# A split-precision expert loop whose h tile is written in place into a PSUM bank

## What is computed

```python
def expert_step(acc, w):
    wg, wu, wd = w                       # 128x512, 128x512, 512x128
    h = jax.nn.silu(x @ wg) * (x @ wu)
    return (acc + h @ wd, None)
acc, _ = jax.lax.scan(expert_step, jnp.zeros_like(x), (Wg, Wu, Wd))
```

## Time and profile before

| | |
|---|---|
| time, median of 3 runs | 551.64 us (551.34 to 551.76) |
| time of the profiled execution | 551.68 us |
| its span | 549.9 us, 8707 instructions |
| TensorE matmuls busy | 541.6 us (98%), 2643 instructions |
| VectorE busy | 442.1 us (80%), 978 |
| ScalarE busy | 347.7 us (63%), 626 |
| GpSimd busy | 164.3 us (30%), 205 |
| granted TensorE clock | 0.999 of full |

### The profile page before, as it was taken

How to read it: one execution, slowest core, us unless ns; L and a number is a source line. 1 busy time by engine, 2 the same in 40 slices (tenths; PEclk the granted TensorE clock), 3 DMA queues, 4 the chain that set the end, 5 groups by cost and what they waited for, 6 DMA issues and landing times.

```text
span 549.9 us, 8707 instructions
## 1 busy us (share of the span) xinstructions
PE 541.6 (98%) x2643; PEld 467.0 (85%) x2643; DVE 442.1 (80%) x978; ACT 347.7 (63%) x626; POOL 164.3 (30%) x205
## 2 busy tenths in 40 slices
PE   9999999999999999999999999999999999999996
PEld 5788888888888888888888888888888888888885
DVE  5689887898768997789877988779976888778666
ACT  6797676756675566755658466675667555655554
POOL 6567784216203360034501335022520033001001
PEclk9999999999999999999999999999999999999999
DMA  6233320210102101111101111021010200010000
GB/s 191 78 121 111 107 65 3 77 45 13 60 0 78 58 20 39 42 35 59 49 10 63 35 41 57 1 76 40 20 40 0 78 20 21 19 40 0 21 0 21
DMA packets 29329, 25.47 MB, mean 46 GB/s; under 512 B 3169, under 2 KB 21986, under 8 KB 29282
## 3 DMA queue, kind: packets, MB, share of 16 engines
q1 hardware_dynamic: 27984, 24.19, 13.8%
q10 hardware_dynamic: 1298, 0.72, 0.5%
HBM read 15.73 MB, written 9.18 MB: 45 GB/s over the span
## 4 chain that ended last, share of the span: by engine, by line
PE 95%; ACT 2%; DVE 1%; issue 1%; POOLq 0%; POOL 0%; DVEq 0%; ACTq 0%
PE gate_ps L1064 10%; PE acc_ps L1067 10%; PE acc_ps L1064 10%; PE gate_ps L1065 10%; PE gate_ps L1067 10%; PE acc_ps L1065 10%; PE up_ps L1064 10%; PE up_ps L1065 10%; PE up_ps L1067 10%; PE att_ps L1121 1%; PE att_ps L1109 1%; PE up_ps L1167 1%; ACT h_hi L627 1%; PE att_ps L1097 1%; PE gate_ps L1167 0%
## 5 line engine op out<-in xcount | busy, mean ns | idle before, releaser
L650 ACT ACTIVATE gs<-gate_ps 128x512 f32<-128x512 f32 x255 | 152.0, 596 | 175.4 <-PE gate_ps L1067 172.3
L874 DVE TENSOR_TENSOR h<-gs,up_ps 128x512 f32<-128x512 f32 x255 | 174.1, 683 | 92.9 <-PE up_ps L1067 90.0
L861 DVE TENSOR_TENSOR h_lo<-h,h_hi 128x512 fp32r<-128x512 f32 x255 | 193.8, 760 | 0.1
L627 ACT ACTIVATE h_hi<-h 128x512 fp32r<-128x512 f32 x255 | 158.9, 623 | 9.4 <-DVE h L874 8.9
L1064 PE MATMUL gate_ps<-x1nT_hi,wg_hi 128*128 128x512 f32 (+1 forms) x254 | 98.7, 388 | 1.7 <-ACT wg_hi L580 0.9
L1067 PE MATMUL acc_ps<-h_lo,wd_hi 128*128 128x512 f32 x254 | 96.4, 379 | 0.2 <-DVE h_lo L861 0.2
L1064 PE MATMUL acc_ps<-h_hi,wd_hi 128*128 128x512 f32 x254 | 96.3, 379 | 0.0
L1065 PE MATMUL acc_ps<-h_hi,wd_lo 128*128 128x512 f32 x254 | 96.3, 379 | 0.0
L1065 PE MATMUL up_ps<-x1nT_hi,wu_lo 128*128 128x512 f32 (+1 forms) x254 | 96.1, 378 | 0.0
L1067 PE MATMUL gate_ps<-x1nT_lo,wg_hi 128*128 128x512 f32 (+1 forms) x254 | 96.1, 378 | 0.0
L1064 PE MATMUL up_ps<-x1nT_hi,wu_hi 128*128 128x512 f32 (+1 forms) x254 | 96.1, 378 | 0.0
(11 more groups left out here) (233 smaller groups left out, 492.8 us busy)
## 6 DMA issues: line engine op xcount, KB each, us to landing
w_raw<-in_L_ffn_Wg_dram SPq DMA_DIRECT2D x8, 256.0 KB, 2.8
w_raw<-in_L_ffn_Wu_dram SPq DMA_DIRECT2D x8, 256.0 KB, 2.6
w_raw<-in_L_ffn_Wd_dram SPq DMA_DIRECT2D x8, 256.0 KB, 3.5
x_in<-in_L_attn_x_dram SPq DMA_DIRECT2D x7, 256.0 KB, 2.9
t_dram_x1n<-t_blk_x1n SPq DMA_DIRECT2D x7, 256.0 KB, 2.0
t_out_x1n<-t_dram_x1n SPq DMA_DIRECT2D x28, 64.0 KB, 1.9
t_dram_acc<-t_blk_acc SPq DMA_DIRECT2D x7, 256.0 KB, 2.3
t_out_acc<-t_dram_acc SPq DMA_DIRECT2D x28, 64.0 KB, 2.0
```

The source lines that it names most:

```text
L627: act.activation(h_hi[s % NH][:, :], h[s % NGU][:, :], ACT.Copy).then_inc(s_hhi, 1)
L650: act.activation(gs[q][:, :], gate_ps[q][:, :], ACT.Silu).then_inc(s_silu, 1)
L861: dve.tensor_tensor(h_lo[s % NH][:, :], h[s % NGU][:, :], h_hi[s % NH][:, :].bitcast(F32), ALU.subtract).then_inc(s_hlo, 1)
L874: dve.tensor_tensor(h[q][:, :], gs[q][:, :], up_ps[q][:, :], ALU.mult).then_inc(s_h, 1)
```

## The change

h loses its tiles in SBUF. VectorE writes gs * up back into the PSUM bank from which it read up. ScalarE makes h_hi and VectorE makes h_lo from that bank. The bank is then free for the next up when h_lo is made, so TensorE's wait before up is on s_hlo instead of s_h; VectorE's waits before h (until h_hi and h_lo of the tile's last user are made) go away.

In the last step the second half of up goes to the attention's bank att_ps, for which TensorE doesn't wait, and the first half of the last sum to up_ps[(STEPS - 3) % NGU].

The splits of the weights are moved: expert e's three tiles are copied at steps 4 (e - 2), + 1 and + 2, and their low parts made one step later. Those of experts 0 and 1 (m up to 5) are made before the first step. GpSimd no longer waits for s_hlo. TensorE waits for the low parts of Wg and of Wu separately, each before its first product.

```diff
-LO_AT = {4: 1, 5: 2, 6: 3, 7: 4, 8: 6, 9: 7, 10: 8, 11: 10, 12: 11, 13: 12, 14: 14, 15: 15, 16: 16, 17: 17, 18: 20,
-         19: 21, 20: 24, 21: 25, 22: 26, 23: 27}
-HI_AT = {m: when - 1 for m, when in LO_AT.items() if m > 5}
+FIRST = 2
...
+        HI_AT = {m: FT * (m // 3 - FIRST) + m % 3 for m in range(3 * FIRST, NW)}
+        LO_AT = {m: when + 1 for m, when in HI_AT.items()}
...
-        h = [sb(f"h{i}", [P, N]) for i in range(NGU)]
...
-        last_up_ps = [up_ps[(STEPS - 1) % NGU], up_ps[(STEPS - 3) % NGU]]
-        last_acc_ps = [att_ps, gate_ps[(STEPS - 2) % NGU]]
+        last_up_ps = [up_ps[(STEPS - 1) % NGU], att_ps]
+        last_acc_ps = [up_ps[(STEPS - 3) % NGU], gate_ps[(STEPS - 2) % NGU]]
...
                     for m, when in LO_AT.items():
                         if first and when == s:
-
-                            pool.wait_ge(s_hlo, s)
                             split_lo(pool, m)
...
             pool.wait_ge(s_f_x1n, J)
-            split_lo(pool, 2)
-            split_lo(pool, 3)
+            for m in range(2, 3 * FIRST):
+                split_lo(pool, m)
...
-                act.activation(h_hi[s % NH][:, :], h[s % NGU][:, :], ACT.Copy).then_inc(s_hhi, 1)
+                act.activation(h_hi[s % NH][:, :], up_ps[s % NGU][:, :], ACT.Copy).then_inc(s_hhi, 1)
...
-                dve.tensor_tensor(h_lo[s % NH][:, :], h[s % NGU][:, :], h_hi[s % NH][:, :].bitcast(F32),
+                dve.tensor_tensor(h_lo[s % NH][:, :], up_ps[s % NGU][:, :], h_hi[s % NH][:, :].bitcast(F32),
                                   ALU.subtract).then_inc(s_hlo, 1)
...
-                    if not (first and s < NGU):
-                        dve.wait_ge(s_hhi, t - since(s, NGU) + 1)
-                        dve.wait_ge(s_hlo, t - since(s, NGU) + 1)
                     q = s % NGU
-                    dve.tensor_tensor(h[q][:, :], gs[q][:, :], up_ps[q][:, :], ALU.mult).then_inc(s_h, 1)
+
+                    dve.tensor_tensor(up_ps[q][:, :], gs[q][:, :], up_ps[q][:, :], ALU.mult).then_inc(s_h, 1)
...
-                if first and f == 0:
-                    pe.wait_ge(s_whi, 3 * e + 2)
-                    pe.wait_ge(s_wlo, 3 * e + 2)
-                for k, ps, s_done, s_free in ((0, gate_ps[q], s_gate, s_silu), (1, up_ps[q], s_up, s_h)):
+                for k, ps, s_done, s_free in ((0, gate_ps[q], s_gate, s_silu), (1, up_ps[q], s_up, s_hlo)):
+                    if first and f == 0:
+                        pe.wait_ge(s_wlo, 3 * e + k + 1)
                     if not (first and s < NGU):
                         pe.wait_ge(s_free, t - since(s, NGU) + 1)
...
-                                                  (1, last_up_ps[i], s_up, s_h)):
-                        pe.wait_ge(s_free, t - 3 + 1 + i)
+                                                  (1, last_up_ps[i], s_up, s_hlo)):
+                        if ps is not att_ps:
+                            pe.wait_ge(s_free, t - 3 + 1 + i)
```

More of the change, by code:

```diff
@@ L639, in last_step @@
                     act.wait_ge(s_h, t + 1 + i)
-                    act.activation(h_hi[r][:, half], h[q][:, half], ACT.Copy).then_inc(s_hhi, 1)
+                    act.activation(h_hi[r][:, half], last_up_ps[i][:, half], ACT.Copy).then_inc(s_hhi, 1)
             def body(b, par, first, nxt, last):
@@ L889, in last_step @@
                     dve.wait_ge(s_silu, t + 1 + i)
-                    dve.tensor_tensor(h[q][:, half], gs[q][:, half], last_up_ps[i][:, half],
+                    dve.tensor_tensor(last_up_ps[i][:, half], gs[q][:, half], last_up_ps[i][:, half],
                                       ALU.mult).then_inc(s_h, 1)
@@ L894, in last_step @@
                     dve.wait_ge(s_hhi, t + 1 + i)
-                    dve.tensor_tensor(h_lo[r][:, half], h[q][:, half], h_hi[r][:, half].bitcast(F32),
+                    dve.tensor_tensor(h_lo[r][:, half], last_up_ps[i][:, half], h_hi[r][:, half].bitcast(F32),
                                       ALU.subtract).then_inc(s_hlo, 1)
```

## The result

The changed kernel takes 563.02 us (median of four runs, 562.79 to 563.20) against 551.63 us; the ratio is 1.0207, with a 95% interval of 1.0189 to 1.0225. The forecast was 563.3 us, with a range of 559.2 to 566.5.

The account below looks back on a forecast made before the run. TensorE was taken as the bound, busy 541.6 of 549.9 us. Image-start stalls 5.4, step-5 stalls 6.1 and first image 0.1 summed to +11.6 us on 551.7, giving 563.3 us, range 559.2 to 566.5.

Parts of the forecast that it names:

- The stalls at s=0 and s=1: First two steps of images 1 to 7: up waits for h_lo of two steps earlier, 14 times, 5.4 us in all.
- The stalls at s=5: Step 5 of images 1 to 6: up waits for h_lo made late by ScalarE's table loads, six times, 6.1 us.
- What a stall costs beyond its lateness: At each TensorE wait: 0.08 us from release to start, plus 0.07 us before the next matmul.
- The price of PSUM: h written to and read from PSUM: taken as no cost; upper bound 0.08 us per stall, 1.6 us for 20.
- the page's rule: Trainium skill's VectorE access overhead, about 125 ns on PSUM against 60 on SBUF: 2.6 us over 20 stalls, time 566.0.
- h_lo without collisions: With one SBUF operand h_lo no longer waits for GpSimd splits: mean from 760 to about 685 ns, none near 1.39 us.
- The first image: Waits that go against new waits of up there: sum +0.1 us, bounds -1.0 to +1.
- up(3) and up(7): First image, up at steps 3 and 7 waits for h_lo: starts 27.25, 1.17 us late, and 36.54, 1.45 us late.
- A dear write: Rival, chance 0.04: writing into the PSUM bank being read doubles h to 1.2 us; about 595 us.
- only one kind of stall: Rival, chance 0.07: only the image-start waits or only the step-5 waits of up appear, 5.4 or 6.1 us; 557.4 us.
- Faster: Rival, chance 0.04: up's wait for h_lo never binds, three first-image waits are gain, 2.65 us; 549.0 us.
- unchanged: Rival, chance 0.02: gains and stalls cancel within 0.2%, 1.1 us, needing stalls of 2.7 us in all.

Follow-up runs that it names:

- the wait alone: Kernel before with one word changed: TensorE's up waits for s_hlo instead of s_h, h stays in SBUF, splits as before; 564.31 us, ratio 1.0230.
- the run with the splits alone: Kernel before with only the new weight-split times, no s_hlo wait on GpSimd, separate TensorE waits; h stays in SBUF; 551.83 us, ratio 1.0003.

## Why the prediction was right, point by point

- *The stalls at s=0 and s=1.* Forecast 14 x 0.385 = 5.4 us; the trace has 7 x (0.40 + 0.35) = 5.3 us, and choosing banks by t took away 5.24. Right, in mechanism and size.
- *The stalls at s=5.* Forecast 6 x 1.02 = 6.1 us; the trace has 6 x 1.00. Identity for Exp took away 7.66, of which 6.0 are these and 1.5 is up(7)'s stall of the first image. Right, and the table loads are the cause.
- *What a stall costs beyond its lateness.* Forecast 0.08 for the release and 0.07 behind it; measured 0.05 and 0.10. The two errors cancel, which is luck: I took the 0.07 from a matmul released by a split, while the one released by h_lo in the same rows, 0.48 us long instead of 0.38, already showed the 0.10.
- *The price of PSUM.* Taken as 0, at most 0.08 per stall. h went from 683 to 693 ns and h_hi from 623 to 593. From the start of one instruction to that of the next, where they follow without a pause, h takes 605 ns (604 before), h_lo 601 (602) and h_hi 478 (520). The rule of the Trainium skill (Perfetto Trace Analysis, section Optimizing Scalar/DVE Operations), which would have made it 65 ns for each of VectorE's two, is not borne out here; its other half, that ScalarE is quicker on PSUM than on SBUF, is: its 42 ns are those from start to start, 520 less 478. The time that I gave for the page's rule, 566.0, should have read 565.9.
- *h_lo without collisions.* Forecast about 685 ns with nothing near 1.39; measured 681 ns, 691 at most. The Trainium skill says the same (SBUF — State Buffer, section Who interferes with whom): an instruction of VectorE with two inputs in SBUF contends with GpSimd's reads, one with a single SBUF input, outside the two-port modes, does not. What I had not seen is that such collisions also filled the later images of the kernel before (12 of h_lo's 20 us); TensorE did not wait for them, so the sum was not touched.
- *The first image.* Forecast +0.1 us, measured +0.18, of which 0.07 lie ahead of step 3 (its gate starts at 25.50 instead of 25.43). Its parts hold too. The changed kernel at up(3) and up(7):

```profile
25.93 0.38 PE L1061 MATMUL gate_ps<-x1nT_lo,wg_hi 128*128 128x512 f32 x1
...
27.30 0.48 PE L1058 MATMUL up_ps<-x1nT_hi,wu_hi 128*128 128x512 f32 x1 [0.99 <-DVE h_lo L859]
```

```profile
34.95 0.38 PE L1061 MATMUL gate_ps<-x1nT_lo,wg_hi 128*128 128x512 f32 x1
...
36.59 0.48 PE L1058 MATMUL up_ps<-x1nT_hi,wu_hi 128*128 128x512 f32 x1 [1.26 <-DVE h_lo L859]
```

  up(3) at 27.30 (forecast 27.25) and up(7) at 36.59 (36.54). The waits for splits at gate(4) and gate(28) and that of down(8) for h_lo are gone.
- *Rivals.* A dear write is refuted by h's 693 ns in the changed kernel, and the wait alone, at 564.31 us, loses as much without it; that only one kind of stall would appear is refuted by the trace of the changed kernel. Faster and unchanged are refuted by the time.

What my working missed only showed in the experiments: I never asked what the new splits would do to an h_lo that is still in SBUF.

## What to carry to other kernels

A buffer that is kept until a later reader is a longer loop for the engine that fills it: compare, for every step and not for a typical one, the time at which the later reader ends with the time at which the filler now starts, and look first at the places where the distance of a rotation is shorter (here 32 steps over three banks) and where one engine is late for a reason of its own (here two table loads). When the bounding engine is 98% busy, 1 us of such lateness in each image is 1 us of the time, however much less busy all the others become. And where VectorE and GpSimd both work from SBUF, moving one engine's work in time changes the other's durations: count them anew.

## What the runs showed of the hardware

- A wait in front of a matmul costs 0.10 us more than the delay of its start: the matmul behind comes 0.32 us after it instead of 0.216. Its weight load stands at the start of the matmul (88.12) and not 0.22 us ahead of it (87.39 for the one at 87.61).
- Stalls of TensorE of 1.15 us (in front of 27.30) and 1.42 us (in front of 36.59) left the granted clock at 1.00. One of 4.85 us was followed by 14 matmuls at 0.50.
- When VectorE's and GpSimd's subtractions, both with all operands in SBUF, overlap, the one that starts second is lengthened: h_lo ends 0.54 to 0.55 us after the split has ended, a split 1.13 to 1.16 us after h_lo, in all 25 overlaps of more than 0.06 us in the first image of the run with the splits alone. So both sides suffer when the splits follow one another without a pause (0.68 to 1.2 us and 1.28 to 1.75), and only h_lo where each split waits for an h_lo and so starts first (1.39).
- VectorE writes in place into a PSUM bank at the price of 10 ns in the duration of an instruction of 512 columns, and of 1 ns from its start to the next. ScalarE's copy reads PSUM 42 ns faster than SBUF, from start to start.
